# Attention and a mixture of experts on one core: table numbers read earlier, the last batch settled in two halves, less padding between scatters

## The chip, the core and the metric

The kernel runs on one core of a Trainium2 chip. The metric is device microseconds (us) of one execution, start to end. The engines are TensorE (PE: matmuls and transposes), VectorE (DVE), ScalarE (ACT), GpSimd (POOL) and SyncE (SP), which issues most of the transfers. Each runs its own list of instructions in order; they meet through semaphores.

## The reference

Eight sequences of 512 tokens of 128 channels pass through causal attention with 16 heads of 64 and rotary embedding, a residual and a layer norm, and then through a mixture of eight experts of which each token takes the best two:

```python
x = _layernorm(x + attention(x, Wq, Wk, Wv, Wo, bo))          # (8, 512, 128)
# experts, for x of the line above:
weights = softmax(x @ gate_w.T + expert_bias)
top_w, top_i = top_k(weights, 2)                               # renormalised
out = sum over e of sparse_w[e] * (gelu(x @ w_up[e].T) @ w_down[e].T)   # 128 -> 512 -> 128
out = (out - mu) * rsqrt(var + 1e-5) + x
x = _layernorm(x + out)
```

## The kernel before

**Attention.** There are 64 units, one for each sequence (called a batch in the code) and each pair of heads. Each engine has a function `attention(u, ...)` that says what it does in unit u: TensorE scores, transposes and the product with the values (`attend`), VectorE the masked maxima and the scaled sum (`scale_y`), ScalarE the exponentials and the copies of the transposed weights (`copy_pt`), GpSimd the rotation. SyncE waits in each unit for a projection and loads the output weights that are needed two units later. Behind the units of a batch its tokens are normalised and routed: VectorE finds the two experts and a slot for each choice, and GpSimd sends the rows by scatter DMAs (`send_row`, 128 rows each, eight for a batch) to `xrows` in memory, where the rows of an expert lie together.

**Experts.** The rows are worked on in 71 tiles of 128 rows of one expert (`TILES`). Two tables say for each tile which rows (`tile_row`) and which expert (`tile_expert`). The first 24 tiles (`EARLY`) are set from the first four batches, in the attention; the others once the last batch is routed. For tile t, SyncE loads the rows (`load_rows`) and, for the first 18, the up weights from memory (`load_weights`, issued four steps after its index: at step t it loads those of tile t - 4, once TensorE has done the up product of tile t - 8). TensorE transposes the rows, multiplies up (`up`, L1127) and down (`down`, L1136), ScalarE does the gelu and the weighting into `ys`, and GpSimd scatters the 128 result rows to `yrows` by token (`send_y`, L814). Behind a scatter GpSimd sets 448 columns to zero that nobody reads (`space`), except behind the last four. While tiles 3 to 11 run, the last batch is routed, so TensorE, VectorE and ScalarE also do its logits (L1021), its exponential, with a table load before and after, and its ranks.

**Numbers.** SyncE needs the numbers in registers. `values` reads a few of a table; `PLACES_AT` and `NUMBERS_AT` say before which tile's loads: rows at 0, 6 and 9, experts at 4, 7 and 10, eight at a time.

**The end.** When all rows of a batch are in `yrows`, SyncE loads them (`load_y`), VectorE adds the two choices and takes two norms in a row: sum, statistics, root, `add_x1`, statistics, root, factors. ScalarE normalises and SyncE writes out. `COMPLETE[b]` says how many tiles must have been sent. The last batch needs all 71; its four blocks of 128 tokens come by four loads (L503), and then all four pass each step together (`sum_last` to `factors`). Its roots are ScalarE's. Blocks 0 and 1 are normalised by ScalarE, 2 and 3 by VectorE (L1870).

In the traces `x1T`, `w_tile`, `hT` and `shared` are tiles of the on-chip memory that hold several things in turn: at the start x transposed, the query and key weights, and the value weights.

## Time and profile before

| | |
|---|---|
| median of 3 runs | 844.44 us (841.27 to 846.9) |
| the profiled execution | 844.71 us, its span 843.0 us |
| mean granted clock of TensorE | 0.987 |
| busy: PE, DVE, ACT, POOL | 812.5, 673.7, 628.8, 558.5 us |
| attention, to the last unit's scores | to about 665 us |
| tiles of the experts | about 681 to 826 us |
| behind TensorE's last product | 826 to 843 us |

The span is from the first to the last instruction; what the execution's time has over it lies before and behind. A busy share says little here, as each stretch has another bound. A row of a timeline is one instruction or a run of equal ones: start, time, engine, line, operation, written from read, and in brackets how long the engine sat idle before it and what ended that.

### The profile page before, as it was taken

What the parts mean: (1) busy time and instruction counts of PE and PEld (TensorE: products, weight loads), DVE (VectorE), ACT (ScalarE), POOL (GpSimd) and SP (SyncE); (2) the same over time, 40 slices, a digit from 0 to 9 for tenths busy, and PEclk for the clock granted to TensorE, in tenths of its full rate; (3) what the DMA queues carried; (4) which work ended last, traced back from release to release, by engine and by line L of the source; (5) the groups of instructions that cost most, each with busy time, mean ns of one, the idle gap of its engine ahead of it and who ended that gap; (6) DMA issues with size and microseconds to landing.
All of it is one profiled execution on the core that took longest, in us unless ns stands there. A gap on an engine that the chain in (4) does not pass through costs nothing.

```text
span 843.0 us, 21026 instructions
## 1 busy us (share of the span) xinstructions
PE 812.5 (96%) x6239; PEld 586.9 (70%) x6239; DVE 673.7 (80%) x2711; ACT 628.8 (75%) x1671; POOL 558.5 (66%) x614
## 2 busy tenths in 40 slices
PE   7999999999999999999999999999999989999991
PEld 4556666666666666666666666666666579999991
DVE  5887798889888988898889988988898754225986
ACT  3677887888788877887887788778877855556575
POOL 5765646456756775667568856765685355989894
PEclk9999999999999999999999999999999998999996
DMA  5111101000100010010001000100022156434524
GB/s 162 32 40 38 51 20 33 8 20 27 39 14 30 27 39 19 23 51 15 26 14 51 14 30 11 51 18 14 14 60 77 48 150 179 137 85 126 157 86 150
DMA packets 54991, 46.03 MB, mean 55 GB/s; under 512 B 6384, under 2 KB 46576, under 8 KB 54880
## 3 DMA queue, kind: packets, MB, share of 16 engines
q1 hardware_dynamic: 50416, 35.63, 14.6%
q0 software_dynamic: 4320, 8.92, 3.1%
q8 instruction: 53, 0.87, 0.4%
q14 instruction: 58, 0.48, 0.2%
q10 hardware_dynamic: 144, 0.13, 0.1%
HBM read 28.39 MB, written 12.08 MB: 48 GB/s over the span
## 4 chain that ended last, share of the span: by engine, by line
PE 91%; POOL 2%; DVE 2%; DMA 2%; issue 1%; ACT 1%; SPq 0%; POOLq 0%; ACTq 0%; DVEq 0%
PE TB L976 18%; PE S_all L929 17%; PE TB L960 14%; PE AO L997 7%; PE S_all L1127 7%; PE AO L856 4%; PE S_all L960 3%; PE TB L1136 3%; PE AO L858 3%; PE AO L1136 3%; PE AO L857 3%; PE AO L920 1%; PE AO L918 1%; PE AO L919 1%; POOL yrows L814 1%
## 5 line engine op out<-in xcount | busy, mean ns | idle before, releaser
L1214 ACT ACTIVATE Pr_all<-Sm,nmax 128x512 f32<-128x512 f32 (+3 forms) x512 | 279.6, 550 | 0.1
L1389 DVE CUSTOM_DVE_ANT_0 Sm<-S_all,causal 128x512 f32<-128x512 f32 (+3 forms) x512 | 220.1, 486 | 72.7 <-PE S_all L929 72.7
L621 POOL TENSOR_TENSOR shared<-shared,sin_t 128x512 f32<-128x512 f32 x63 | 80.5, 1277 | 173.5 <-DVE shared L1369 173.5
L1226 ACT ACTIVATE PT<-TB 128x1024 f32<-128x1024 f32 x185 | 131.0, 742 | 63.5 <-PE TB L960 63.5
L929 PE MATMUL S_all<-kT,qT 64*128 64x512 f32 (+3 forms) x1024 | 166.7, 443 | 1.6 <-POOL kT L624 1.1
L976 PE MATMUL TB<-PT,shared 128*64 128x128 f32 x992 | 149.8, 441 | 2.2 <-ACT PT L1226 0.3
L1410 DVE SCALAR_TENSOR_TENSOR x_acc<-AO,rinv,x_acc 128x128 f32<-128x128 f32 x504 | 141.7, 344 | 2.4 <-PE AO L997 0.2
L960 PEld LDWEIGHTS TB<-ident,Pr_all 128*128 128x128 f32 x1000 | 107.8, 141 | 38.3 <-ACT Pr_all L1214 21.1
L960 PE MATMUL TB<-ident,Pr_all 128*128 128x128 f32 x1000 | 133.6, 277 | 0.5 <-ACT PT L1226 0.5
L929 PEld LDWEIGHTS S_all<-kT,qT 64*128 64x128 f32 x1024 | 78.9, 187 | 70.9 <-issue 54.1
L1214 ACT ACTIVATION_READ_ACCUMULATOR Pr_all<-Sm,nmax 128x1 f32 x512 | 97.2, 190 | 0.0
L976 PEld LDWEIGHTS TB<-PT,shared 128*64 128x64 f32 x992 | 59.3, 136 | 51.4 <-issue 32.9
L616 POOL TENSOR_TENSOR qT<-shared 128x512 f32<-128x512 f32 x64 | 82.5, 1289 | 9.1
L997 PEld LDWEIGHTS AO<-wo,OT 64*128 64x128 f32 x1008 | 65.6, 187 | 31.2 <-issue 31.2
L666 POOL DMA_INDIRECT xrows<-pay,slot x64 | 65.1, 1018 | 32.5 <-DVE pay L1560 14.0
L613 POOL TENSOR_TENSOR shared<-shared,sin_t 128x512 f32<-128x512 f32 x64 | 82.1, 1283 | 6.6 <-DVE shared L1362 6.6
L624 POOL TENSOR_TENSOR kT<-shared 128x512 f32<-128x512 f32 x63 | 80.3, 1275 | 9.3 <-POOL shared L621 0.4
L997 PE MATMUL AO<-wo,OT 64*128 64x128 f32 x1008 | 67.5, 273 | 0.0
L1232 ACT ACTIVATE OT<-TB 128x512 f32<-128x512 f32 x62 | 37.0, 597 | 26.7 <-PE TB L976 26.7
L1203 ACT ACTIVATE shared<-AO 128x512 f32<-128x512 f32 x62 | 37.1, 598 | 25.9 <-PE AO L920 19.0
L856 PE MATMUL AO<-x_hi,wqk 128*128 128x512 f32 x112 | 54.0, 482 | 0.0
L1226 ACT ACTIVATE PT<-S_all 128x512 f32<-128x512 f32 (+1 forms) x66 | 39.2, 598 | 18.3 <-PE S_all L960 15.1
(296 smaller groups left out, 1426.7 us busy)
## 6 DMA issues: line engine op xcount, KB each, us to landing
wo<-in_wo SPq DMA_DIRECT2D x64, 64.0 KB, 1.8
PT<-yrows SPq DMA_DIRECT2D x7, 512.0 KB
w_tile<-in_wup SPq DMA_DIRECT2D x10, 256.0 KB
xt<-xrows SPq DMA_DIRECT2D x32, 65.0 KB
x_acc<-in_x SPq DMA_DIRECT2D x8, 256.0 KB
wdown<-in_wdown SPq DMA_DIRECT2D x8, 256.0 KB, 3.1
pay<-pay SPq DMA_DIRECT2D x8, 256.0 KB
x_acc<-pay SPq DMA_DIRECT2D x8, 256.0 KB
```

What stands on the lines that cost most here:

```text
L613: nc.gpsimd.tensor_tensor(q_rot, q_rot, sin_t[:, :], ALU.mult).then_inc(q_mul, 1)
L616: nc.gpsimd.tensor_tensor(qT[p][:, :], q_cos, q_rot, ALU.add).then_inc(q_ready, 1)
L621: nc.gpsimd.tensor_tensor(k_rot, k_rot, sin_t[:, :], ALU.mult).then_inc(k_mul, 1)
L856: nc.tensor.matmul(bank[:, :], high, x_hi[batch % 2][:, :], start=True, stop=False)
L929: nc.tensor.matmul(SB[2 * (group % 2) + h][:, at:at + (qb + 1) * P], qT[p][half, qb * P:qb * P + P], kT[p][half, 0:(qb + 1) * P], start=Tr ...
L960: last = nc.tensor.transpose(bank, Pr[j][:, kb * P:kb * P + P], ident[:, :])
L976: last = nc.tensor.matmul(o_bank(u)[D * h:D * h + D, kb * P:T], V[u // VS % 2][:, kb, u % VS * P + D * h:u % VS * P + D * h + D], PT[p][:, ...
L997: last = nc.tensor.matmul(y_bank(u)[h][:, i * P:i * P + P], OT[p][half, i * P:i * P + P], wo[p][half, :], start=True, stop=True)
L1214: nc.scalar.activation(Pr[j][:, 0:n], Sm[j], ACT.Exp, bias=nmax[:, j:j + 1], scale=-1.0, accum_out=rsum[p][:, h * QB + qb:h * QB + qb + 1] ...
L1226: last = nc.scalar.activation(PT[p][:, :, 0:qb + 1, qb * P:qb * P + P], source, ACT.Copy)
L1389: nc.vector.tensor_tensor_reduce(out=Sm[j], in0=SB[2 * (group % 2) + h][:, at:at + n], in1=causal[:, T - n:T], scale=-0.125, scalar=HUGE, ...
L1410: last = nc.vector.scalar_tensor_tensor(out=tile, in0=y_bank(u)[h][:, i * P:i * P + P], scalar=rinv[:, h * QB + i:h * QB + i + 1], in1=til ...
```

## The change

- **Start.** SyncE issues cos, the second half of the first query and key weights, sin and the value weights ahead of the other weights; the gate's weights, its bias and the output bias come last.
- **Numbers.** The numbers of the first 24 row places and 18 experts are read in units 50 to 55 of the attention.
- **Last attend.** Unit 63's product goes to a bank of `TB`, no longer to that which held unit 62's output. It no longer waits for VectorE's reading of that one, and waits for its transposed weights in three steps. TensorE waits for that reading before the down product of tile 0 instead.
- **Padding.** None behind the first, third, fifth and seventh of the last batch's row scatters, nor behind the results of tiles 65 and 66.
- **Halves.** The table of tiles gets one more class, so that the rows of the last batch's first two blocks lie in the first 67 tiles. These blocks are loaded once 67 tiles are sent, the others once all are. TensorE adds the first half's two choices by products with the identity into banks of `S_all`; each half passes the steps by itself. ScalarE takes blocks 0 to 2, VectorE block 3, and the last batch goes out in three writes.
- **Table.** `final_table` on VectorE works out two classes at once, in one more step.

```diff
-CLASSES = B - FRONT + 2
+PARTS = ((0, QB // 2), (QB // 2, QB))
+CLASSES = B - FRONT + 1 + len(PARTS)
-COMPLETE = [EARLY + E] * HEAD + [tiles_begun(max(FRONT, b + 1)) for b in range(HEAD, B)]
+COMPLETE = [EARLY + E] * HEAD + [tiles_begun(max(FRONT, b + 1)) for b in range(HEAD, B - 1)]
+PART_COMPLETE = [TILES - (QB - end) * K for first, end in PARTS]
...
-POOL_NORMS, LAST_NORMS = (0, 0, 0, 1, 1, 1, 0, 0), 2
+POOL_NORMS, LAST_NORMS = (0, 0, 0, 1, 1, 1, 0, 0), 1
...
-PLACES_AT = {0: (0, 8), 6: (8, 16), 9: (16, EARLY)}
-PLACES_AT.update({t: (t, min(t + 8, TILES)) for t in range(EARLY, TILES, 8)})
-NUMBERS_AT = {4: (0, 8), 7: (8, 16), 10: (16, W_LOADS)}
+
+EARLY_PLACES_AT = {50: (0, 8), 52: (8, 16), 54: (16, EARLY)}
+EARLY_NUMBERS_AT = {51: (0, 8), 53: (8, 16), 55: (16, W_LOADS)}
+PLACES_AT = {t: (t, min(t + 8, TILES)) for t in range(EARLY, TILES, 8)}
...
-                    for dst, src in ((gate_t, gate_h), (ebias_t, ebias_h)):
+                    sp.dma_start(cos_t[:, :], cos_h).then_inc(rope_in, 16)
+                    sp.dma_start(w_stage[0][:, 2 * P:4 * P], wqk_h[:, 2 * P:4 * P]).then_inc(wqk_in[0], 16)
+                    sp.dma_start(sin_t[:, :], sin_h).then_inc(rope_in, 16)
+                    sp.dma_start(wv, wv_h).then_inc(wv_in, 16)
+                    for i in range(1, PAIRS // 2):
+                        sp.dma_start(w_stage[i][:, :], wqk_h[:, i * 4 * P:(i + 1) * 4 * P]).then_inc(wqk_in[i], 16)
+                    for dst, src in ((bo_t, bo_h), (gate_t, gate_h), (ebias_t, ebias_h)):
                         sp.dma_start(dst[:, :], src).then_inc(consts_in, 16)
-                    for dst, src in ((cos_t, cos_h), (sin_t, sin_h)):
-                        sp.dma_start(dst[:, :], src).then_inc(rope_in, 16)
-                    for i in range(PAIRS // 2):
-                        at = 2 * P if i == 0 else 0
-                        sp.dma_start(w_stage[i][:, at:4 * P], wqk_h[:, i * 4 * P + at:(i + 1) * 4 * P]).then_inc(wqk_in[i], 16)
-                        if i == 0:
-                            sp.dma_start(wv, wv_h).then_inc(wv_in, 16)
-                    sp.dma_start(bo_t[:, :], bo_h).then_inc(consts_in, 16)
...
+                if u in EARLY_PLACES_AT:
+                    sp.wait_ge(tables_ready, 1)
+                    load_places(*EARLY_PLACES_AT[u])
+                if u in EARLY_NUMBERS_AT:
+                    of = EARLY_NUMBERS_AT[u]
+                    experts.extend(values(mybir.EngineType.SP, tile_expert, of[0], of[1] - of[0], E - 1))
+
+            rows, experts = [], []
+
+            def load_places(first, end):
+
+                rows.extend(values(mybir.EngineType.SP, tile_row, first, end - first, SPARES))
...
+            def load_last(part):
+
+                b, complete = B - 1, PART_COMPLETE[part]
+                for t in range(complete - XT, complete):
+                    sp.wait_ge(ys_sent[t % XT], 16 * (t // XT + 1))
+                y_v = yrows[Y0:Y0 + B * T * K, :].rearrange("(t p k) c -> p t (k c)", p=P, k=K)
+                for i in range(*PARTS[part]):
+                    sp.dma_start(y_buf(b)[:, i:i + 1, :], y_v[:, QB * b + i:QB * b + i + 1, :]).then_inc(y_last_in[i], 16)
...
-            for b in range(HEAD + 1):
+            for b in range(HEAD):
                 send_out(b)
-            load_y(B - 1)
+            load_last(0)
+            send_out(HEAD)
+            load_last(1)
...
-                if t < TILES - 4:
+                if t < TILES - 6:
                     space()
                 if t == LAST_SENDS:
                     rows_ready(B - 1)
                     for choice in range(QB * K):
                         send_row(B - 1, choice)
-                        space()
+                        if choice % 2:
+                            space()
 
...
-                pe.wait_ge(pt_ready, 3 * u + 2)
+                pe.wait_ge(pt_ready, 3 * u + (1 if u == UNITS - 1 else 2))
                 if u == UNITS - 2:
                     pe.wait_ge(maxed, BLK * UNITS)
-                if u == UNITS - 1:
-                    pe.wait_ge(y_read, 2 * u)
                 for kb in reversed(range(QB)):
+                    if kb == 2 and u == UNITS - 1:
+                        pe.wait_ge(pt_ready, 3 * u + 2)
                     if kb == 1:
...
+            for i in range(*PARTS[0]):
+                pe.wait_ge(y_last_in[i], 16)
+                y = y_buf(B - 1)
+                nc.tensor.matmul(SB[i][:, 0:C], ident[:, :], y[:, i, 0:C], start=True, stop=False)
+                nc.tensor.matmul(SB[i][:, 0:C], ident[:, :], y[:, i, C:K * C], start=False, stop=True).then_inc(last_summed, 1)
...
             norm2_of(3, 0, act_blocks(3))
+            norm2_of(4, 0, act_blocks(4))
             root_half(KNOWN)
-            norm2_of(4, 0, act_blocks(4))
+            root_sum_part(0)
             norm2_of(5, 0, act_blocks(5))
-            norm2_of(KNOWN, 0, act_blocks(KNOWN))
-            root_sum(B - 1)
-            root_half(B - 1)
-            norm2_of(B - 1, 0, act_blocks(B - 1))
+            norm2_of(KNOWN, 0, 2)
+            root_half_part(0)
+            root_sum_part(1)
+            norm2_of(KNOWN, 2, act_blocks(KNOWN))
+            norm2_part(0)
+            root_half_part(1)
+            norm2_part(1)
...
+            def sum_part(part):
+
+                blocks, y = range(*PARTS[part]), y_buf(B - 1)
+                for i in blocks:
+                    if part == 0:
+                        dve.wait_ge(last_summed, i + 1)
+                    else:
+                        dve.wait_ge(y_last_in[i], 16)
+                        nc.vector.tensor_tensor(sum_of(part, i), y[:, i, 0:C], y[:, i, C:K * C], ALU.add).then_inc(summed, 1)
+                        dve.wait_ge(summed, B + i - blocks[0])
+                    last = nc.vector.bn_stats(st2[:, 0, NT - QB + i, :], sum_of(part, i))
...
             finish_norm(KNOWN)
+            sum_part(0)
             factors(KNOWN)
-            sum_last()
-            invert_sum(B - 1)
-            add_x1(B - 1)
-            stats_half(B - 1)
-            factors(B - 1)
-            dve.wait_ge(factors_ready, factors_of(B - 1))
+            add_part(0)
+            sum_part(1)
+            factors_part(0)
+            add_part(1)
+            factors_part(1)
...
```

Of SyncE at the start, before:

```order
L426 DMA x1T<-in_xT 128x512
L428 DMA gate_t<-in_gate 128x8
L428 DMA ebias_t<-in_ebias 128x8
L430 DMA cos_t<-in_cos 128x512
L430 DMA sin_t<-in_sin 128x512
L433 DMA w_tile<-in_wqk 128x256
L435 DMA shared<-in_wv 128x1024
L433 DMA w_tile<-in_wqk 128x512
```

and now:

```order
L436 DMA x1T<-in_xT 128x512
L437 DMA cos_t<-in_cos 128x512
L438 DMA w_tile<-in_wqk 128x256
L439 DMA sin_t<-in_sin 128x512
L440 DMA shared<-in_wv 128x1024
L442 DMA w_tile<-in_wqk 128x512
L442 DMA hT<-in_wqk 128x512 x2
L444 DMA bo_t<-in_bo 128x128
L444 DMA gate_t<-in_gate 128x8
```

The second half of the first weights and the value weights stand two places further up, the small loads of the gate behind all weights.

SyncE at the start of the tiles, before, from the up weights of tile 4 (`w_tile0`) to those of tile 6 (`qT0`), with the rows of tiles 8 and 9 (`cos_t`); L393 reads the table's numbers, an ISA row sets an address or a register:

```order
L537 ISA [waits up_done]
L537 DMA w_tile0<-in_wup 128x512
L530 ISA [waits k_mul,q_read,q_mul,k_read,scored]
L530 DMA cos_t<-xrows 128x130
L393 TENSOR_LOAD table_r
L393 ISA x16
L537 ISA [waits up_done]
L537 DMA w_tile1<-in_wup 128x512
L530 ISA
L530 DMA cos_t<-xrows 128x130
```

and now the same place:

```order
L562 ISA [waits up_done]
L562 DMA w_tile0<-in_wup 128x512
L555 ISA [waits k_mul,q_read,q_mul,k_read,scored]
L555 DMA cos_t<-xrows 128x130
L562 ISA [waits up_done]
L562 DMA w_tile1<-in_wup 128x512
L555 ISA
L555 DMA cos_t<-xrows 128x130
```

with the reads of these numbers in the attention, for instance in unit 50, between the loads of output weights:

```order
L495 DMA x_acc<-in_x 128x4x128
L403 TENSOR_LOAD table_r [waits tables_ready]
L403 ISA x16
L455 DMA wo1<-in_wo 128x128 [waits y_done]
```

The read of eight row numbers has left the place between the weights of tiles 4 and 5.

VectorE at the end, before, from batch 6's second addition to the last batch's first sum:

```order
L1803 SCALAR_TENSOR_TENSOR Pr_all<-Pr_all,Sm,x_acc 128x128 x4
L1811 BN_STATS st<-Pr_all 128x6 x4
L1815 BN_AGGR mv<-st 128x2 x4
L1835 RECIPROCAL Sm<-Sm 128x4
L1821 SCALAR_TENSOR_TENSOR Sm<-mv,Sm 128x4
L1846 TENSOR_TENSOR Pr_all<-PT 128x128
L1848 BN_STATS st<-Pr_all 128x6
```

and now from the first half's statistics to the second half's first:

```order
L1909 BN_STATS st<-S_all 128x6 x2
L1913 BN_AGGR mv<-st 128x2 x2
L1890 RECIPROCAL Sm<-Sm 128x4
L1883 SCALAR_TENSOR_TENSOR Sm<-mv,Sm 128x4
L1920 RECIPROCAL Sm<-Sm 128x2
L1924 SCALAR_TENSOR_TENSOR Pr_all<-S_all,Sm,x_acc 128x128 x2
L1929 BN_STATS st<-Pr_all 128x6 x2
L1933 BN_AGGR mv<-st 128x2 x2
L1907 TENSOR_TENSOR Pr_all<-PT 128x128
L1909 BN_STATS st<-Pr_all 128x6
```

The first half's statistics, norm and second statistics stand before the second half's rows are waited for (L1907).

## Rows read from the trace of the kernel before

**Rows 1.** Chain from 655 to 712 us: start us, us, what.

```profile
676.93 1.13 DVE x_acc L1410 x4
...
690.31 2.77 DMA w_tile<-in_wup
...
696.00 1.51 PE S_all L1021 x8
...
703.29 1.28 ACT L1299
...
705.88 1.13 PE S_all L1127 x8
...
708.01 0.89 PE S_all L1127 x8
...
709.90 0.89 PE S_all L1127 x8
```

**Rows 2.** Chain from 740 to 845 us.

```profile
828.66 2.24 DMA yrows<-OT,cos_t
...
830.98 2.17 DMA PT<-yrows
```

**Rows 3.** SyncE's timeline from 655 to 720 us: start us, us, issue.

```profile
685.12 0.33 SPq L530 DMA_DIRECT2D cos_t<-xrows  x1
690.31 0.34 SPq L537 DMA_DIRECT2D w_tile<-in_wup  x1
```

**Rows 4.** Stretches: us, busy of five engines, TensorE's granted clock, DMA share, GB/s.

```profile
691.00:694.00 3.00, 0.93 (x8) 0.87 (x8) 0.96 (x4) 0.35 (x2) 2.59 (x4) 1.00 0.62 181
697.00:700.00 3.00, 3.00 (x15) 3.00 (x15) 1.14 (x6) 0.55 (x2) 1.45 (x2) 0.50 0.94 295
```

**Rows 5.** ScalarE's timeline from 674 to 700 us.

```profile
676.47 1.57 ACT L1226 ACTIVATE PT<-S_all 128x768 f32<-128x768 f32 x3 [0.68 <-PE S_all L960]
```

**Rows 6.** Timelines of GpSimd and ScalarE from 709 to 829 us.

```profile
709.74 0.97 POOL L814 DMA_INDIRECT yrows<-OT,xt  x1 [0.17 <-issue]
...
711.37 0.98 POOL L666 DMA_INDIRECT xrows<-pay,slot  x1 [0.17 <-issue]
...
822.79 1.41 POOL L814 DMA_INDIRECT yrows<-OT,xt  x1 [0.17 <-issue]
...
827.39 0.96 POOL L814 DMA_INDIRECT yrows<-OT,cos_t  x1 [0.30 <-issue]
...
823.80 0.37 ACT L1306 ACTIVATE OT<-AO,cos_t 128x128 f32<-128x128 f32 x1 [0.30 <-PE AO L1136]
...
825.61 0.37 ACT L1306 ACTIVATE OT<-AO,cos_t 128x128 f32<-128x128 f32 x1 [0.17 <-issue]
```

**Rows 7.** Timeline from 0 to 14 us.

```profile
3.64 0.43 SPq L435 DMA_DIRECT2D shared<-in_wv  x1
...
8.99 1.12 PE L853 MATMUL AO<-x1T,w_tile 128*128 128x512 f32 x2 [2.08 <-DMA w_tile<-in_wqk]
...
10.07 1.64 DVE L1380 TENSOR_TENSOR kT<-shared 128x512 f32<-128x512 f32 x1
10.38 0.19 PEld L911 LDWEIGHTS S_all<-shared,x1T 128*128 128x128 f32 x1 [0.24 <-DMA shared<-in_wv]
...
13.48 0.70 PE L929 MATMUL S_all<-kT,qT 64*128 64x512 f32 x2
```

**Rows 8.** Timeline from 823.5 us to the end.

```profile
833.17 0.29 DVE L1846 TENSOR_TENSOR Pr_all<-PT 128x128 f32<-128x128 f32 x1 [2.60 <-DMA PT<-yrows]
...
835.40 0.38 DVE L1852 BATCH_NORM_AGGREGATE mv<-st 128x2 f32<-128x6 f32 x4
...
836.36 1.14 DVE L1803 SCALAR_TENSOR_TENSOR Pr_all<-Pr_all,Sm,x_acc 128x128 f32<-128x128 f32 x4
...
838.85 0.30 ACT L1317 ACTIVATE Sm<-mv,eps_half 128x4 f32<-128x4 f32 x1 [2.74 <-DVE mv L1815]
...
839.59 0.88 ACT L1327 ACTIVATE Pr_all<-Pr_all,Sm 128x128 f32<-128x128 f32 x2 [0.44 <-DVE Sm L1821]
```

More of the change, by code:

```diff
@@ L202, in build_block @@
         pay = [sb(f"pay{i}", [P, QB, K, ROW]) for i in range(2)]
-        count, counted_t = (sb(n, [P, E]) for n in ("count", "counted_t"))
+        count, counted_t = sb("count", [P, len(PARTS), E]), sb("counted_t", [P, E])
         head, full, used, later, part = (sb(n, [P, E]) for n in ("head", "full", "used", "later", "part"))
-        begun = [sb(f"begun{i}", [P, E]) for i in range(CLASSES)]
+        begun_all = sb("begun_all", [P, CLASSES, E])
+        begun = [begun_all[:, i, :] for i in range(CLASSES)]
         left = sb("left", [P, E + 1])
@@ L1318, in root_half, with root_sum_part, root_half_part, norm2_part @@
                                      bias=eps_half[:, 0:1]).then_inc(root2, 1)
+            def root_sum_part(part):
+                first, end = PARTS[part]
+                act.wait_ge(var1, B + part)
+                nc.scalar.activation(sd2[:, part_roots(0, part)], mv2[:, 0, NT - QB + first:NT - QB + end, 1], ACT.Sqrt,
+                                     bias=eps_sum[:, 0:1], scale=4.0).then_inc(root1, 1)
+            def root_half_part(part):
+                first, end = PARTS[part]
+                act.wait_ge(var2, B + part)
+                nc.scalar.activation(sd2[:, part_roots(1, part)], mv2[:, 1, NT - QB + first:NT - QB + end, 1], ACT.Sqrt,
+                                     bias=eps_half[:, 0:1]).then_inc(root2, 1)
+            def norm2_part(part):
+                act.wait_ge(factors_ready, factors_of(B - 1) + part)
+                first, end = PARTS[part]
+                for n in range(NT - QB + first, min(NT - QB + end, NT - LAST_NORMS)):
+                    ins = nc.scalar.activation(f_acc[:, n, :], f_acc[:, n, :], ACT.Identity, bias=shift2[:, n:n + 1], scale=root_of(1, n))
+                ins.then_inc(normed2, 1)
             def act_blocks(b):
[L1321 removed]
+                return QB - POOL_NORMS[b]
             def norm2_of(b, first, end):
@@ L1849, in sum_last, with add_part @@
                 last.then_inc(gathered1, 1)
-                dve.wait_ge(gathered1, B)
-                for i in range(QB * b, QB * b + QB):
-                    last = nc.vector.bn_aggr(mv2[:, 0, i, :], st2[:, 0, i, :])
+                dve.wait_ge(gathered1, B + part)
+                for i in blocks:
+                    last = nc.vector.bn_aggr(mv2[:, 0, NT - QB + i, :], st2[:, 0, NT - QB + i, :])
                 last.then_inc(var1, 1)
+            def add_part(part):
+                blocks, of = range(*PARTS[part]), part_roots(0, part)
+                dve.wait_ge(root1, part + 1)
+                nc.vector.reciprocal(rstd2[:, of], sd2[:, of]).then_inc(inverted1, 1)
+                dve.wait_ge(inverted1, part + 1)
+                for i in blocks:
+                    n = NT - QB + i
+                    last = nc.vector.scalar_tensor_tensor(out=f_acc[:, n, :], in0=sum_of(part, i), scalar=root_of(0, n),
+                                                          in1=x_acc[:, n, :], op0=ALU.mult, op1=ALU.add)
+                last.then_inc(added, 1)
+                dve.wait_ge(added, B + part)
+                for i in blocks:
+                    last = nc.vector.bn_stats(st2[:, 1, NT - QB + i, :], f_acc[:, NT - QB + i, :])
+                last.then_inc(gathered2, 1)
+                dve.wait_ge(gathered2, B + part)
+                for i in blocks:
+                    last = nc.vector.bn_aggr(mv2[:, 1, NT - QB + i, :], st2[:, 1, NT - QB + i, :])
+                last.then_inc(var2, 1)
```

76 lines of the change are left out of this document (38 added, 38 removed).

## The prediction

> **What bounds the kernel now.** I read the chain of work that ended last in order of time, at the border between attention and experts and over the last 100 us. There one sees which engine hands on to which. Through the attention the chain lies on TensorE. At the border it leaves TensorE for three things: VectorE's last scaling until 678.06, then a DMA of up weights from 690.31 to 693.08, then ScalarE's table loads until 704.57 [rows 1]. From 705.88 TensorE runs a tile each 1.89 us. For the last tiles the chain lies on GpSimd's scatters, and from 828.66 on scatter, load and the settling of the last batch, to 843.0 [rows 2]. The profiled run took 844.71 for a span of 843.0, so 1.71 lie around the span, and it stands 0.27 above the median of 844.44. All sums are made against that run.
>
> **Numbers loaded in attention.** SyncE reads the row and expert numbers eight at a time in front of the loads they belong to. Before tile 9 it reads eight row numbers: its issues stand at 685.12 and 690.31, so after the issue's own 0.33 it was away for 4.86 us [rows 3]. The issue at 690.31 is the weight tile 5, and nothing else held it: it needs the up products of tiles 0 and 1, and TensorE was past these. The DMA took 2.77, and TensorE started tile 5 at 693.13. In the 3 us from 691 it was busy for 0.93 at a clock of 1.00, so it idled for 2.07; from 697 to 700 the granted clock was 0.50, the 1.2 GHz level [rows 1, 4]. What that costs comes from the rows: up of tile 5 to up of tile 9 took 705.88 - 693.13 = 12.75 us [rows 1]. At the full clock, 2.4 GHz, four tiles take 4 x 1.89 = 7.56, the logits half of 1.51 = 0.75, and the wait for ScalarE's table loads about 0.9 (an estimate: two loads of 1.28 [rows 1] and two short activations, together some 3.4, of which TensorE, that runs two tiles ahead, hides all but the rest). That is 9.2, so 3.55 us are the clock's. If the gap is gone I expect the clock to stay, since up to it it was full. Term: 2.07 + 3.55 = 5.6 us; 2.07 alone if the clock falls anyway.
> The Trainium skill (TensorE: Matmul & The Clock Gate, Part 1) says that the default clock is the halved one, that sustained activity releases it and idling takes it back, and that the gate looks at times of its own, not the kernel's. By the first half of that rule the term is the whole 5.6; by the second it is partly luck, and the rival below has its price.
> The reads themselves move to units 50 to 55. There SyncE waits for a projection in each unit and issues one load of output weights, needed two units later. The 64 units take some 665 us, so a unit has over 10, and two 20. Even 4.86 more leaves over 10 us, so I cost the reads at nothing; what hides them is TensorE's own work on the two units. Behind a read stand the copies of a batch's rows and the next load of weights; should one be late, TensorE pays.
>
> **The last attend.** Unit 63's product waited until VectorE had read unit 62's output, at 678.06 [rows 1], because it wrote the same bank. It now writes another one. What ends last there next is ScalarE's copies of the transposed weights, 676.47 to 678.04 [rows 5]. The first three of its ten parts of 128 columns run before that (one, then two; the product lasted 2.37, so 0.7 of it), and seven after. Start 678.2, less 0.7 done ahead: 0.75 us earlier with the smaller hand-over. VectorE's scaling of unit 63 and all the routing behind it follow by the same amount. The added wait at tile 1 is for a scaling that ended long before. Between 0 and 1.27, as if it had begun at 676.93.
> Up product of tile 9, and with it TensorE and GpSimd from there, move by 0.75 + 2.07 + 3.55 = **6.4 us**.
>
> **The padding.** GpSimd is never idle from 709.74 on: it sends each tile's results some 3 us behind ScalarE and catches up slowly. The last tile's were ready at 825.61 + 0.37 = 825.98 and went at 828.66 [rows 2, 6]. A padded send takes 711.37 - 709.74 = 1.63, a bare one 828.66 - 827.39 = 1.27 [rows 2, 6], so each pad taken away is 0.36. Six go: four behind the last batch's rows, two at the end, 2.16 us. GpSimd alone would send the last tile at 828.66 - 6.4 - 2.16 = 820.1. But TensorE's end moves by 6.4 only: tile 68, ready at 823.80 + 0.37, is ready at 817.8 [rows 6]. Sent 0.15 later, two bare sends behind it make 820.5. So the last scatter starts **8.2 us** earlier, and TensorE has become the second bound beside GpSimd.
> Against this stands what a send can cost: the one at 822.79 took 1.41 in place of 0.96 while VectorE added a batch's rows [rows 6]. If all six bare ones were stretched so, 6 x 0.45 = 2.7 would be lost and the pads' gain gone. I take the 0.96, since four bare sends at the end show it. The skill (SBUF - State Buffer, "two separate sides") explains such a stretch by VectorE locking GpSimd out of the port it writes descriptors through; this trace bears it out at that one send and not at the bare ones.
>
> **The start.** TensorE got its second weights at 8.99 after an idle, then ran without a gap to the first scores at 13.48 [rows 7]. Now they are issued two places earlier and land earlier. What is late next is the value weights: they held the weight load at 10.38, and were issued at 3.64; now at about 2.69, 0.95 earlier, behind the same large loads. Then the product follows at once and not 0.43 later. I take 1.2 us. Below, 0 (bandwidth the same, landing the same). Above, the first rotated keys end at 11.71, which leaves 13.48 - 11.71 = 1.77. Moving the bias and gate loads back costs nothing: they are first used in unit 1, two dozen instructions of VectorE later.
>
> **The tail by halves.** The first half of the last batch needs the tiles up to 66, whose send goes 828.66 - 822.79 = 5.9 us before the last, by the same sum 5.5 now; 2.24 to land and 2.17 to load [rows 2] put its sums about when TensorE has ended, and the second half's rows follow. VectorE sat idle for 2.60 before 833.17 [rows 8]. The first half is some 2.2 of work: half of the per-block work below without the additions. It fits if batch 6's load comes earlier by as much as the last one, since it hangs on GpSimd's sends too; if VectorE moves with TensorE only, by 6.4 and not 8.2, it is 1.4 late. I take the first. What remains behind the last load is a half. From 833.17 to 835.40 there are four blocks' sums and statistics, 2.23, now 1.11. From 835.40 to 836.36, 0.96, of which 0.38 is four aggregations: now 0.77. The first half's factors come in between: 0.1. From 836.36 to 838.85, 2.49 of work per block: now 1.25. The root to the norm, 0.74, stays, and ScalarE is still at four norms of others: 0.15 more. The norms and the outputs, 3.41 from 839.59 to the end, lose one block on each engine, 0.3: now 3.1 [rows 8]. Together 1.11 + 0.77 + 0.1 + 1.25 + 0.74 + 0.15 + 3.1 = 7.2 against 9.83, so **2.6 us**. Three outputs in place of two, and one more step in the last table, lie beside other work; if VectorE isn't free in time, up to 1.4 of it is lost. TensorE's four added products come behind its last tile, so they delay nothing.
>
> **Sum.** 1.2 + 8.2 + 2.6 = 12.0. 844.71 - 12.0 = 832.7, and 0.3 less for the median: **832.4**. The terms' bounds give 830.5 to 835.
>
> **Rivals.** *The clock falls all the same* somewhere between 675 and 705, where TensorE still has short gaps and waits for ScalarE. For it: the three runs of before spread by 5.6 us, as if it came in one and not the other. Against it: 1.00 before the gap. TensorE's end then moves by 6.4 - 3.55 = 2.85; it is the bound, so the last scatter starts at 820.5 + 3.5 = 824.0: 832.4 + 3.5 = 835.9.
> *The tiles' weights stay late*, since what held SyncE was not the numbers but its own instructions arriving (the trace shows 4.86 between two issues, and not what filled it). Then the 5.6 stay; tile 68 is ready at 823.4 and the last scatter starts at 826.1, 2.5 earlier; 1.2 + 2.5 + 2.6 = 6.3: 838.1.
> *Slower:* the reads hold SyncE in the attention. It decides once a read, with its load, lasts longer than the two units, 20 us; a late load would stall TensorE in six units, and each stall of over 2 us brings 3.5 of half clock as in rows 4. Six of 5.6 are 34, and 832.4 + 34 = 866. The rows show 4.86, a quarter of what is needed, so it is very unlikely, but nothing else reaches over to the other side.
> *More than I count:* the start gives its 1.77, the tail is as short as it can be: 830.
>
> **How the numbers follow.** Forecast 0.60 (830.5 to 835), the clock falls 0.17, the weights stay late 0.10, more 0.10, slower 0.03. The range 829.8 to 837.5 leaves out the slower one, the weights that stay late and the far ends of the others. Within 1% of before, which is about what a measurement can tell from no change, begins at 836.0: the forecast, the better case and half of the clock's case are below. Faster 0.79, same 0.18, slower 0.03.
>
> **What would show it.** SyncE issues weight tile 5 soon after the up product of tile 1, at about 682; TensorE has no gap at 691 and a granted clock of 1.00 through 694 to 702; up of tile 9 at about 698.3 (6.4 and the start's 1.2 earlier); the last scatter at about 819.3; the first scores at 12.3; from the first load of the second half to the end 7.2 us. Wrong would be: a new wait of TensorE for ScalarE at 698, which takes the clock down; sends of GpSimd of 1.2 and more; VectorE still busy with the first half when the second is loaded.

## The result, and the profile after

| | median | range | runs |
|---|---|---|---|
| before | 843.38 us | 840.98 to 846.9 | 21 |
| after | 845.87 us | 844.63 to 848.7, one run of 2848 left out | 21 |

The ratio of after to before is 1.0033, with a 95% interval of 1.0023 to 1.0043. I had forecast 832.4, and the change is a third of a per cent slower. The profiled execution has a span of 843.1 us, against 843.0 before.

Nearly all that I had forecast for the parts did come. The start, from the timeline:

```profile
12.31 1.13 PE L955 MATMUL S_all<-kT,qT 64*128 64x512 f32 x4 [0.50 <-DVE kT L1432]
```

The first scores run at 12.31, as forecast, and not at 13.48 [rows 7]; over all runs the gain is smaller, as told below. The next place is the border to the experts. First SyncE's issues, then the same stretches as in [rows 4]:

```profile
682.23 0.33 SPq L562 DMA_DIRECT2D w_tile<-in_wup  x1
```

```profile
691.00:694.00 3.00, 3.00 (x30) 3.00 (x29) 1.14 (x6) 1.27 (x4) 1.82 (x3) 1.00 0.91 255
697.00:700.00 3.00, 2.27 (x21) 2.05 (x20) 2.38 (x17) 2.40 (x8) 0.71 (x1) 1.00 0.59 185
```

The up weights of tile 5 go out at 682.23 and not at 690.31 [rows 3]. TensorE has no gap from 691 to 694 and keeps the full clock from 697 to 700. The up product of tile 9 starts at 698.84, before it was 705.88 [rows 1]: 7.0 us earlier; forecast were 7.6. Up to here the forecast holds.

The loss comes behind it. These are the stretches that follow, with the same columns (busy of TensorE, its weight loads, VectorE, ScalarE and GpSimd, then the clock):

```profile
706.00:710.00 4.00, 3.69 (x33) 3.40 (x32) 0.00 (x0) 0.87 (x2) 3.36 (x6) 1.00 0.51 141
710.00:714.00 4.00, 1.34 (x8) 1.02 (x8) 0.31 (x2) 0.60 (x2) 3.29 (x4) 1.00 0.67 157
714.00:720.00 6.00, 2.74 (x11) 2.38 (x12) 0.00 (x0) 0.90 (x3) 5.42 (x8) 0.53 0.56 145
720.00:724.00 4.00, 3.50 (x17) 3.23 (x17) 0.86 (x2) 2.04 (x6) 2.83 (x4) 0.50 0.34 87
```

From 710 to 720 TensorE works 4.1 of 10 us, and its clock falls to the half. GpSimd is busy all the time. The chain of waits over the same stretch has pieces that it can't name:

```profile
710.41 3.33 another core or an unknown queue
...
714.53 4.34 another core or an unknown queue
```

The timelines of ScalarE, TensorE and VectorE say what these pieces are. In brackets stand the idle time before an instruction and what ended it:

```profile
710.04 0.37 ACT L1339 ACTIVATE OT<-AO,cos_t 128x128 f32<-128x128 f32 x1 [2.71 <-PE TB L1162]
713.76 0.60 ACT L1308 ACTIVATE hT<-S_all 128x512 f32<-128x512 f32 x1 [3.35 <-remote]
...
718.90 0.37 ACT L1339 ACTIVATE OT<-TB,sin_t 128x128 f32<-128x128 f32 x1 [4.37 <-remote]
721.19 0.60 ACT L1308 ACTIVATE x_next<-S_all 128x512 f32<-128x512 f32 x1 [1.93 <-remote]
```

```profile
706.49 0.27 PE L1138 MATMUL S_all<-ident,places 128*2 128x128 f32 x1
706.60 1.08 PE L1153 MATMUL S_all<-xT,w_tile 128*128 128x128 f32 x8
...
707.63 1.06 PE L1162 MATMUL TB<-wdown,x_next 128*128 x8
708.52 1.06 PE L1153 MATMUL S_all<-xT,qT 128*128 128x128 f32 x8
...
714.67 2.05 PE L1153 MATMUL S_all<-xT,kT 128*128 128x128 f32 x8 [2.14 <-ACT xT L1303]
...
719.52 2.07 PE L1162 MATMUL TB<-wdown,hT 128*128 x8 [2.59 <-ACT OT L1339]
```

```profile
710.79 0.20 DVE L1641 CAST table_e<-S_all 2x48 int32<-2x48 f32 x1 [5.04 <-remote]
```

TensorE and ScalarE work in the order of the tiles, so the n-th gelu belongs to the n-th up product. Counted so, the gelu of 713.76 (L1308) is tile 13's, and it waits for nothing but its up product. That started at 706.60 and took 1.08, so it was over at 707.68: the signal took effect 6.1 us late. The gelu of 721.19 is tile 14's, with the product of 708.52: 11.6 us late. The weighting at 718.90 (L1339), which reads `TB`, waits for nothing but its down product, from 707.63 to 708.69: 10.2 us late. VectorE's row at 710.79 needs the small product of 706.49 and is 4.0 us late. "Remote" means that the profile has the increase of the semaphore just before the wait ends, but no instruction that ended near it: for the gelu of 713.76 the increase is recorded at 713.74. So it is not ScalarE's own instruction that comes late. TensorE in turn waits for these ScalarE results (2.14 and 2.59), so engines that wait for nothing of GpSimd's here stand still. GpSimd itself doesn't stand: it sends on without a pause.

```profile
704.15 0.96 POOL L691 DMA_INDIRECT xrows<-pay,slot  x1 [0.17 <-issue]
705.42 0.96 POOL L691 DMA_INDIRECT xrows<-pay,slot  x1 [0.30 <-issue]
...
707.03 0.96 POOL L691 DMA_INDIRECT xrows<-pay,slot  x1 [0.17 <-issue]
```

Two row sends follow each other 1.27 apart, and the next pair begins 2.88 after the first: 1.44 a send on the mean. With a padding behind each it would be 1.62.

Two simple readings fall by the same trace. One is that ScalarE has to wait for its instructions: from 703 to 717 the trace has no packet of an instruction queue. The other is that the DMA engines are full, or that the scatters pile up in them. The DMA share of the last column but one is 0.67 and 0.56 from 710 to 714 and from 714 to 720, where the run with full padding, below, has 0.89 and 0.49 and no pause. And the last packet of each row send started at most 3.1 us after the send, with full padding at most 4.3.

At the end of the kernel the chain is again as forecast:

```profile
831.38 2.22 DMA yrows<-OT,cos_t
...
834.06 2.29 DMA PT<-yrows
...
836.37 0.30 DVE Pr_all L1907
...
837.84 0.62 DVE Pr_all L1924 x2
```

From the last scatter to the end are 843.1 - 831.38 = 11.7 us, and before 843.0 - 828.66 = 14.3 [rows 2]: the halves give 2.6. But the last scatter starts 2.7 later than before and not 8.2 earlier. So the case has one question: what makes the signals late between 706 and 722?

### The profile page after: what moved, and what is told of

Same layout as the page of the kernel before. It is cut to its first block, busy times and chain, and to the rows that moved or that the text cites. A ratio compares the mean times of both kernels' runs of the same rounds, so it can differ in the third digit from the quotient of the medians.

```text
span 843.1 us, 21055 instructions
## 1 busy us (share of the span) xinstructions
PE 814.3 (97%) x6247; PEld 587.8 (70%) x6247; DVE 673.5 (80%) x2714; ACT 629.6 (75%) x1674; POOL 555.9 (66%) x610
## 4 chain that ended last, share of the span: by engine, by line
PE 80%; POOL 8%; issue 6%; DVE 2%; ACT 1%; DMA 1%; another core or an unknown queue 1%; SPq 0%; POOLq 0%; DVEq 0%
PE TB L1002 18%; PE S_all L955 17%; PE TB L986 14%; PE AO L1023 7%; POOL yrows L839 7%; PE AO L882 4%; PE S_all L986 3%; PE AO L884 3%; PE AO L883 3%; POOL shared L857 2%; PE AO L946 1%; PE AO L944 1%; PE AO L945 1%; PE S_all L1153 1%; PE AO L879 1%
## 5 line engine op out<-in xcount | busy, mean ns | idle before, releaser
L1002 PE MATMUL TB<-PT,shared 128*64 128x128 f32 x1008 | 152.4, 441 | 2.3 <-ACT PT L1259 0.3
L1259 ACT ACTIVATE PT<-S_all 128x512 f32<-128x512 f32 (+1 forms) x66 | 39.2, 597 | 18.1 <-PE S_all L986 14.3
```

The source lines that it names most:

```text
L1002: last = nc.tensor.matmul(o_bank(u)[D * h:D * h + D, kb * P:T], V[u // VS % 2][:, kb, u % VS * P + D * h:u % VS * P + D * h + D], PT[p][:, ...
L1259: last = nc.scalar.activation(PT[p][:, :, 0:qb + 1, qb * P:qb * P + P], source, ACT.Copy)
```

## The experiments

**Theory A**: the row sends with half of the padding cause it. **Theory B**: the new timing does, since the last batch's row sends now meet the pad stores and weight loads of SyncE at another moment. The first four runs each undo or make one part.

### Full padding behind the row sends

```diff
                         send_row(B - 1, choice)
-                        if choice % 2:
-                            space()
+                        space()
```

> The changed kernel with the padding put back behind every one of the last batch's eight row sends (alone the half padding undone). Theory A, the unpadded pairs of scatters hold up the signals of the other engines: no pause of TensorE between 706 and 724, up of tile 13 to up of tile 17 about 7.6 us in place of 18.6, four pads of 0.36 more on GpSimd; time about 833.9 (the 832.4 that I forecast and 1.44), at most 836. Theory B, the pause comes with the earlier experts (the row scatters now meet the pad stores and the weight loads at another time), whatever the padding: the pause stays, time 844 to 847.

Measured: 835.44 us (4 runs), ratio to before 0.9935 (0.9918 to 0.9951). The same stretches:

```profile
710.00:714.00 4.00, 3.54 (x32) 3.35 (x31) 0.76 (x2) 2.27 (x6) 3.66 (x6) 1.00 0.89 232
714.00:720.00 6.00, 6.00 (x56) 6.00 (x56) 1.64 (x2) 3.40 (x9) 5.32 (x8) 1.00 0.49 125
720.00:724.00 4.00, 4.00 (x38) 4.00 (x38) 1.51 (x3) 2.27 (x6) 3.66 (x5) 1.00 0.53 132
```

The pause is gone. In this profile no gelu or weighting between 695 and 815 was held up by more than half a microsecond behind its product. The four paddings that I had priced at 0.36 us each are worth 8.3 us by the ratios (1.0033 - 0.9935 = 0.0098) and 8.7 by the profiled spans (843.1 and 834.4). Theory A holds, and this version beats both kernels. It stays short of what I expected; its tail shows a part of why, in ScalarE's and GpSimd's timelines:

```profile
818.26 0.60 ACT L1307 ACTIVATE hT<-S_all 128x512 f32<-128x512 f32 x1 [1.35 <-PE S_all L1152]
```

```profile
814.76 0.97 POOL L839 DMA_INDIRECT yrows<-OT,xt  x1 [0.17 <-issue]
...
817.32 0.96 POOL L839 DMA_INDIRECT yrows<-OT,xt  x1 [0.32 <-issue]
820.28 0.96 POOL L839 DMA_INDIRECT yrows<-OT,cos_t  x1 [2.00 <-ACT OT L1338]
...
822.90 0.96 POOL L839 DMA_INDIRECT yrows<-OT,cos_t  x1 [0.31 <-issue]
```

Three unpadded tile sends stand from 814.76, and then ScalarE has been idle for 1.35 when it gets TensorE's signal, 1.25 after the product's end at 817.02, and GpSimd waits 2.00 for ScalarE. This is the same thing on a small scale, and the last scatter starts at 822.90 in place of the 820.7 of my sum (819.3 and four paddings).

### Half padding alone, in the kernel before

```diff
                         send_row(B - 1, choice)
-                        space()
+                        if choice % 2:
+                            space()
```

> The kernel before with one edit: padding behind every second of the last batch's row sends only. Theory A: a pause of about 10 us at the row scatters, between 711 and 730, of which GpSimd's lag of some 3 us hides a part; the last scatter some 7 us later, time about 850, at least 847. Theory B: no new pause, four pads of 0.36 less on GpSimd, which is the bound there: about 842.5, within 1% of before.

Measured: 850.3 us (4 runs), ratio 1.0099 (1.0072 to 1.0127), so 8.3 us slower with that one line. The chain shows the pieces without a name again, a third one of 2.57 at 721.44 among them:

```profile
714.81 2.57 another core or an unknown queue
...
718.16 2.88 another core or an unknown queue
```

Theory A holds in the old timing too, and theory B falls.

### Numbers loaded in the attention alone

```diff
+EARLY_PLACES_AT = {50: (0, 8), 52: (8, 16), 54: (16, EARLY)}
+EARLY_NUMBERS_AT = {51: (0, 8), 53: (8, 16), 55: (16, W_LOADS)}
...
+                if u in EARLY_PLACES_AT:
+                    sp.wait_ge(tables_ready, 1)
+                    load_places(*EARLY_PLACES_AT[u])
```

> The kernel before with one edit: the row and expert numbers of the first tiles are loaded in units 50 to 55 of the attention. Theory A: the gap at 691 and the low clock at 697 to 705 are gone and nothing takes their place; the experts start 5.6 us earlier and GpSimd, which sends in series, follows in whole: 838 to 839. Theory B: the earlier experts meet the row scatters and the pause of the changed kernel appears: 845 to 850.

Measured: 838.9 us (10 runs), ratio 0.9968 (0.9953 to 0.9982). No pause at the row sends, so theory B falls here too. In the profiled execution the span is 837.0 and thus 6.0 below that of before; by the medians it is 2.4. The two don't agree, and the second execution of the kernel before, below, says why.

### No padding behind the row sends

```diff
                         send_row(B - 1, choice)
-                        if choice % 2:
-                            space()
```

> The changed kernel with no padding at all behind the last batch's row sends. Theory A: all eight scatters follow each other at 1.27, the pause is at least as long as that of the changed kernel, time 846 or more. Theory B: the pause is what it is, four pads less: 844 to 846, and the pause starts no earlier.

Measured: 845.97 us (4 runs), ratio 1.0067 (1.0048 to 1.0087), where half of the padding gave 1.0033. By the ratios that is 2.9 us more, by the spans 0.9 (844.0 and 843.1). The chain has 4.75 without a name at 706.36 and 8.18 at 711.50. The pause starts earlier and is longer, and the tile sends resume 1.5 us sooner (714.16 and 715.68). What is lost is thus not in proportion to the paddings taken away: the first four cost 8.3 us by the ratios, the other four 2.9.

This run also shows that it isn't the signals alone. TensorE's down product of 711.76 has eight equal parts, and nothing but the weights just loaded stands between them. The last two of them:

```profile
714.67 0.37 PE L1160 MATMUL AO<-wdown,hT 128*128 x1 [1.75 <-issue]
716.10 0.37 PE L1160 MATMUL AO<-wdown,hT 128*128 x1 [1.06 <-issue]
```

They start 1.43 apart, and the load of weights between them stands 0.7 from either. With full padding the parts follow each other at 0.11. Such gaps within a product, of 0.7 or 1.4 us, stand in four of the six profiles that have a pause, the changed kernel's among them (at 712.26), and in none of the others. In a pause TensorE itself is held, then, where it waits for no other engine.

The next four ask what it is in the sends: two that follow each other at once (A1), or the mean rate (A2), and whether it takes the row sends at all.

### Two paddings behind each pair

```diff
                         if choice % 2:
                             space()
+                            space()
```

> The changed kernel with two paddings behind every second row send in place of one: the sends stay in unpadded pairs, but the mean distance is some 1.75 us, more than with full padding (1.63). If two sends that follow each other at 1.27 are what holds up the signals (theory A1), the pause stays: 844 to 849. If it is the mean rate of the sends (theory A2), the pause is gone: 833 to 835 (plus the 1 us for the longer row sends, if GpSimd is the bound).

Measured: 836.38 us (4 runs), ratio 0.9924 (0.9896 to 0.9952). GpSimd's sends, and TensorE in the same stretch:

```profile
704.50 0.96 POOL L691 DMA_INDIRECT xrows<-pay,slot  x1 [0.17 <-issue]
705.77 0.96 POOL L691 DMA_INDIRECT xrows<-pay,slot  x1 [0.30 <-issue]
...
707.91 0.96 POOL L691 DMA_INDIRECT xrows<-pay,slot  x1 [0.16 <-issue]
```

```profile
710.00:714.00 4.00, 3.54 (x29) 3.15 (x28) 0.90 (x2) 1.79 (x5) 3.47 (x6) 1.00 0.95 261
714.00:720.00 6.00, 6.00 (x56) 6.00 (x55) 1.60 (x3) 3.54 (x10) 5.13 (x8) 1.00 0.58 145
```

The pairs are as bare as in the changed kernel (705.77 - 704.50 = 1.27), but two of them take 3.41, so 1.70 a send, and there is no pause: TensorE is as busy as with full padding (3.54 and 6.00), though four signals take effect 0.9 to 1.4 us late. A1 falls. The time is 1.4 above the range that I had set for this case.

### A short padding behind each row send

```diff
-SPACE = 448
+SPACE, SHORT = 448, 64
...
                         send_row(B - 1, choice)
-                        if choice % 2:
-                            space()
+                        space(SHORT)
```

> The changed kernel with a short padding (64 columns in place of 448) behind every one of the eight row sends: no two sends are unpadded, but the distance is only some 1.40 us, below the mean of the pairs (1.45). Theory A1 (a bare pair is the cause): no pause, about 833 to 835. Theory A2 (the mean rate): the pause is there, 844 to 848.

Measured: 846.83 us (9 runs), ratio 1.0049 (1.0031 to 1.0067). Each send has a padding behind it, and they stand 1.30 apart (705.41 and 706.71). ScalarE's timeline:

```profile
715.63 0.37 ACT L1338 ACTIVATE OT<-AO,cos_t 128x128 f32<-128x128 f32 x1 [7.62 <-remote]
720.05 0.60 ACT L1307 ACTIVATE hT<-S_all 128x512 f32<-128x512 f32 x1 [4.05 <-remote]
```

One wait lasts 7.62 us, and its product was over 9.0 us before; for the second row it is 12.4. It is the rate that decides. Over how many sends the mean is to be taken isn't shown, and all these runs change the distance by the same memsets; a pause of another kind between the sends wasn't tried.

### Eight unpadded tile sends in the middle, and four

Both have full padding behind the row sends; tiles 24 to 31, and in the second run 24 to 27, are sent without.

```diff
-                if t < TILES - 6:
+                if t < TILES - 6 and not 24 <= t < 32:
                     space()
```

> The kernel with full row padding (changed otherwise), and eight unpadded sends of tile results, tiles 24 to 31, in the middle of the experts, where SyncE has no pad stores. If unpadded sends hold up signals whatever they carry and whatever runs beside them: a pause of several us at about 735 to 750, which GpSimd's lag does not hide since TensorE is late, and 840 to 846. If the row sends or the pad stores beside them are needed for it: no pause, 835.4 as with full row padding, or a little less.

> Full row padding, and four unpadded sends (tiles 24 to 27) in the middle of the experts in place of eight. With eight, ScalarE saw TensorE's signal of 748 only at 755, and the first late one came with the third unpadded send. If what piles up is in proportion to the unpadded sends in a row: a signal at most some 1 to 2 us late, hidden by nothing but short, 835.4 to 837. If any unpadded run in this stretch brings the whole pause: 841 to 843.

Measured: 842.39 us for eight (10 runs), ratio 1.0000 (0.9986 to 1.0015), and 842.64 us for four (10 runs), ratio 1.0003 (0.9990 to 1.0016). Against 0.9935 with padding that is 5.5 us more, for either. The stretch of the first, by ScalarE, TensorE and GpSimd:

```profile
747.81 0.60 ACT L1307 ACTIVATE hT<-S_all 128x512 f32<-128x512 f32 x1 [1.22 <-PE S_all L1152]
...
755.01 0.37 ACT L1338 ACTIVATE OT<-TB,sin_t 128x128 f32<-128x128 f32 x1 [6.44 <-remote]
```

```profile
747.02 1.06 PE L1161 MATMUL TB<-wdown,hT 128*128 x8
...
755.64 2.07 PE L1161 MATMUL TB<-wdown,hT 128*128 x8 [4.66 <-ACT OT L1338]
```

```profile
744.96 0.97 POOL L839 DMA_INDIRECT yrows<-OT,xt  x1 [0.17 <-issue]
746.24 0.96 POOL L839 DMA_INDIRECT yrows<-OT,xt  x1 [0.30 <-issue]
...
752.58 0.96 POOL L839 DMA_INDIRECT yrows<-OT,cos_t  x1 [0.31 <-issue]
756.17 0.96 POOL L839 DMA_INDIRECT yrows<-OT,sin_t  x1 [2.63 <-ACT OT L1338]
```

The weighting at 755.01 needs the down product of 747.02, which was over at 748.08: 6.9 us late. No row send and no pad store stands here. GpSimd's seventh unpadded send ended at 753.54. The eighth, of tile 31, needs this very weighting, so GpSimd stood idle itself, and 1.5 us later the signal was there. With four unpadded sends the longest delay is 7.5 us. I had thought that four would cost a quarter or so of eight; they cost the same, so the expectation for the four was wrong in its likelier half. In this stretch GpSimd is behind and has sent at 1.62 to 1.90 with hardly a wait for 40 us; my reading, not tested, is that there is no room left, and any run at 1.27 goes over.

### Padding of 352 columns

```diff
-SPACE = 448
+SPACE = 352
```

> All of the changed kernel, padding behind every send but the last, and each padding 352 columns in place of 448: a send every 1.55 us in place of 1.63. By the rate theory the limit lies between 1.45 (pauses) and 1.63 (none). If it is below 1.55: no pause, GpSimd catches up with TensorE and the last scatter starts at 820.5 to 821.5: 833.5 to 834.5. If it is above: a pause at the row sends, 842 or more.

Measured: 840.43 us (12 runs, 837.17 to 841.99), ratio 0.9981 (0.9965 to 0.9996). The distance is 1.54 (701.02 and 702.56). In the profile signals are late at the row sends and in the middle of the experts. The longest wait of ScalarE in either place:

```profile
716.28 0.37 ACT L1338 ACTIVATE kT<-AO,sin_t 128x128 f32<-128x128 f32 x1 [2.12 <-PE TB L1161]
...
748.60 0.37 ACT L1338 ACTIVATE OT<-AO,cos_t 128x128 f32<-128x128 f32 x1 [1.95 <-remote]
```

The down products of these two weightings were over at 711.89 and 744.96, so the signals were 4.4 and 3.6 us late; the profile names the wrong product for the first. ScalarE waits for 1 to 2 us at a time, and no wait is as long as those of the pauses. Neither half of the expectation holds as it stands, and against 0.9923 with 448 columns it costs 5 us. The edge is soft. At 1.54 most signals that ScalarE waits for at the row sends are late, by 1.5 to 4.4 us; at 1.62 a single one is still late now and then, by 1.2 us at most (at 720.91 in the kernel before).

### Padding behind the last tile sends too

```diff
-                if t < TILES - 6:
+                if t < TILES - 1:
                     space()
```

> The changed kernel with full padding behind the last batch's row sends and also behind the tile sends up to the last but one (the changed kernel leaves it out behind the last six, the kernel before behind the last four). Theory A, extended: unpadded sends in a row hold up signals wherever they stand, so in the run with full row padding they cost 2.0 us at the end (GpSimd waited 2.00 for ScalarE before the send at 820.28, ScalarE 1.35 for TensorE at 818.26). Padded, TensorE's end at about 819.6 is the bound and the last scatter starts at 820.5 to 821.2 in place of 822.90: 833.4, 1.7 to 2.4 less than full row padding alone (835.4). Rival: the end is no more than GpSimd's serial sends, five pads of 0.36 more: 837.

Measured: 836.03 us (6 runs), ratio 0.9923 (0.9900 to 0.9946), no better than with full row padding alone as far as the intervals tell. The late signals of the tail are gone: ScalarE's last weighting starts at 820.33 and not at 820.93. But now GpSimd's own paddings hold the last scatter, which starts at 822.92. Both halves of the expectation were half right, and they cancel.

### The new order of the first loads, beside the numbers

The edit is the part of the diff in `attention_loads` above, on top of the kernel with the numbers.

> The kernel before with two parts of the change: the numbers loaded in units 50 to 55 and the new order of the first loads. The new order is worth the 1.2 that I forecast: 837.7, 1.2 below numbers alone (838.9), first scores at 12.3. Rival: what the start gains is lost on the way, 838.9.

Measured: 838.74 us (9 runs), ratio 0.9958 (0.9941 to 0.9974), where numbers alone had 0.9968. A gain of 1 us isn't resolved by these intervals, and one pair of profiles isn't enough for it either: the first scores start at 12.21 here and at 12.43 with numbers alone. More profiles together say more, in the next section.

### The kernel before once more

> The kernel before once more, for a second profile. If the half clock at 697 to 700 comes in some executions and not in others, the span may be near 839.5 with a clock of 1.00 there (3.5 less than 843.0); if it comes each time, the span is 842 to 844 with the clock at 0.50.

Measured: one execution of 841.73 us, span 840.0. The stretches of [rows 4], for this execution:

```profile
691.00:694.00 3.00, 1.15 (x10) 1.15 (x11) 0.75 (x2) 0.06 (x1) 2.83 (x4) 1.00 0.72 201
697.00:700.00 3.00, 3.00 (x30) 3.00 (x29) 0.34 (x3) 2.72 (x6) 1.66 (x4) 1.00 0.96 289
```

TensorE has the same gap from 691 to 694 as in the first profile (busy 1.15 of 3 us), and then the full clock and not the half one. From up of tile 5 to up of tile 9 it takes 702.51 - 692.85 = 9.7 us in place of 12.75 [rows 1]. The span is 3.0 shorter. The run with half padding in the kernel before, which has the same reads of numbers, lies between: the clock is at 0.56 from 694 to 697 and at 1.00 again from 697, and the four tiles take 11.1. So the half clock that I had put down to the gap comes in some executions and not in others, and not for the same time. This execution also has a late signal at its end, 2.07 "remote" before ScalarE's last weighting, 1.9 us behind its product: the kernel before already paid now and then for its four unpadded sends there.

## Why the prediction was wrong

**The padding** is the step that failed: "so each pad taken away is 0.36. Six go: [...] 2.16 us." The arithmetic on GpSimd's own line was right; the sends did go 1.27 apart. Its other side was missing. I named one cost of unpadded sends, a stretched send of 1.41, and bounded it at 2.7 us. The bound came from GpSimd's own instructions alone, and that was the wrong row to take: the cost falls on TensorE and its signals to ScalarE and VectorE, which took effect up to 11.6 us late. By the ratios half padding costs 8.3 us in the new timing and 8.3 in the old, where I had put a gain of 1.44. I had no row of eight scatters at 1.27 while TensorE was busy, but I overlooked one of three: in the kernel before row sends start at 685.61 and 686.87 and a tile send at 688.13, and tile 3's gelu at 688.48 comes 0.9 us behind its product. In all fourteen profiles this gelu is 0.7 to 2.6 late, beside sends 1.26 apart. Before, of the tile sends only the last four were unpadded, from 824.86 on, and TensorE's last product ended at 825.58. I let "four bare sends at the end show it" stand for a stretch in which every signal counts. None of my rivals had this mechanism; the slower one, reads that hold SyncE in the attention, didn't come. My first sign of being wrong, a new wait of TensorE for ScalarE that takes the clock down, did come, but at 714.67 and not at 698, and with this cause that I hadn't named.

Perfetto Trace Analysis (DMA Instruction — SWDGE) in the Trainium skill says that the end that the profiler gives for such a DMA is when the last descriptor has been written, not when the transfer is done. The trace agrees: the first packets of the row sends in the changed kernel start 1.5 to 2.1 us after the send, when its 0.96 are over. So the 0.96 us, and the 1.27 from one to the next, don't tell what a dense stream of sends costs the others; the runs put the distance that costs them little at some 1.6 us.

**The numbers** were right as a mechanism: weight tile 5 at 682.23, no gap at 691, and TensorE 7.0 us earlier at tile 9 where 7.6 were forecast. The size holds for the profiled execution (span 837.0 against 843.0). Against the median it is too large. The clock's share, 3.55, measures 3.1 (12.75 less the 9.7 of the second execution, where my sum had 9.2 for the full clock), and it comes in only a part of the executions of before. I had seen the spread of 5.6 us in the three runs and used it for a rival of the changed kernel; it belonged to the kernel before. I set "0.3 less for the median", where it was up to 3. The Trainium skill (TensorE: Matmul & The Clock Gate, Part 1), which I cited, says that the gate looks at times of its own; the two executions of before, with nearly the same gap and two clocks behind it, agree.

**The start** is where one pair of profiles misleads. Before and after give 13.48 - 12.31 = 1.17 at the first scores, as forecast (1.2). Over all profiled executions the old order has 13.48, 12.91, 13.28 and 12.43, a mean of 13.03, and the new one ten between 12.12 and 12.90, a mean of 12.43: 0.6. The two ranges overlap, so that is an estimate. The row of 13.48 was at the slow end.

**The last attend**: from the first scores to the up product of tile 0 the five executions without it take 667.2 to 667.5, mean 667.34, and the nine with it 666.4 to 666.9, mean 666.50. So 0.84, where the term was 0.75.

**The tail by halves**: forecast 2.6, measured 2.6 in the changed kernel (14.3 to 11.7), and 834.4 - 822.90 = 11.5 with full padding. VectorE was done with the first half's second statistics at 835.65, just before the second half's first block was added at 835.72, so the hand-over held, with nothing to spare.

**The last scatter**: "TensorE has become the second bound beside GpSimd" was right in the version with full padding: there it starts at 822.90, 5.8 earlier than before. My sum gave 8.2 less 1.44, and the start's 1.2: 8.0. In between lie 2.2. TensorE was 6.6 ahead of before at the up product of tile 9, where I had 7.6, 5.9 at tile 17, and 4.7 at its last product; 1.25 of what it lost on the way is the late signal of 818.26.

**The sum.** With full padding my forecast is a ratio of 833.9 / 844.44 = 0.9875, and 0.9935 was measured, 5 us less. By my reading up to 3 are the half clock, 1 to 2 the late signals of the tail and 0.6 the start; no run takes these apart. The other 8.3 us and the 1.44 that I had counted as a gain are the padding's, and they made a gain into a loss.

**Open.** The runs show on what it depends (the rate of GpSimd's scatters, whatever rows they carry) and on whom it falls (TensorE's signals to others, and TensorE itself). What it is that the signals and TensorE wait for is not shown; neither the load of the DMA engines nor the arrival of instructions explains it. Whether the number of rows of a scatter counts or their bytes isn't shown either: a send of fewer rows or columns wasn't tried.

## What to carry to other kernels

An instruction on an engine with slack can slow engines that never wait for it. Price a denser stream of GpSimd's scatters by a stretch of the trace in which such a stream runs beside work on the critical path, and if there is none, put the loss of a whole stall into the range. Padding that looks like waste between scatters sets their rate. In this kernel they have to stay some 1.6 us apart where the other engines hand on to each other, and it can be thinned out only where nobody waits for a signal any more. And if the kernel before spreads by some us, look at two of its executions before a term is built on what one of them shows.

## What the runs showed of the hardware

- Scatters of 128 rows of 512 or 520 bytes by GpSimd at a mean distance of 1.27 to 1.44 us made signals of TensorE take effect 3 to 12 us late at ScalarE, and 4 us late at VectorE. At 1.54 they were late by up to 4.4 us, at 1.62 to 1.70 by 1.4 us at most and mostly not at all. In the changed kernel ScalarE's results reached TensorE within 0.3 us meanwhile.
- In four of the six profiles with such a pause TensorE also stood for 0.7 or 1.4 us between two parts of one product (714.67 and 716.10 without padding).
- In the middle of the experts four such sends in a row cost as much as eight (842.64 and 842.39 us).
- In these waits the chain says "another core or an unknown queue", on a kernel of one core. This is how the profile shows a signal that takes effect long after its event.
- Where TensorE stood for several us because of it, the half clock came with it (a mean of 0.53 of full from 714 to 720 in the changed kernel, and 0.50 behind). The waits of 1 to 2 us with 352 columns left it at 1.00. The gap of some 2 us at 691 brought it in two of three profiles of kernels with the old reads, until behind 701 in one and until 697 in the other.
